# Graph attention, graph convolution and LSTM on one core: the ramp of the attention stage laid out anew, and stores within the last LSTM round

## The chip, the cores and the metric

The kernel runs on one core of a Trainium2 chip. The metric is device time in microseconds (us) of one execution; lower is better.

## What is computed

32 graphs of 256 nodes with 128 features each (fp32, 4.19 MB) share one adjacency matrix. Each of two layers normalises its input and adds its result to it:

```python
h = jnp.maximum(_layernorm(x, axis=-1), 0.0)
x = x + gat(h, adj, W, a)   # e = leaky(s1_i + s2_j), masked by adj, softmax over j, times h W
h = jnp.maximum(_layernorm(x, axis=-1), 0.0)
x = x + gnn(h, adj, Wg0, bg0, Wg1, bg1, Wih, Whh, bih, bhh)
# gnn: two graph convolutions h = relu(adj @ (h Wg + b)); then for p = 1, 2, 3, 4 every run of
# p nodes goes through a p-step LSTM, whose last hidden state replaces the run's last node
```

## The kernel before, in words

All of x stays in SBUF as `xs`, 64 tiles of 128 nodes. The unit of work is a pair of graphs: four tiles, 512 columns; there are 16 pairs (`PAIRS`). PE is the matrix engine, DVE the vector, ACT the scalar engine, POOL is GpSimd, SP issues transfers. Each runs a hand-written program in its own order, and semaphores are all that ties them: a wait holds everything behind it on its engine.

**Attention stage** (`phase_a`). A software pipeline of ticks. In tick t, ACT normalises pair t (L448), PE transposes it (L908), and ACT copies it to `hT` (L474). In the tick behind that, PE makes its products with W (L898) and its scores S (L902, once the scores before are read); DVE masks S by `adj_neg`, takes row maxima (L642) and applies the leaky slope (L674). Two, three and four ticks behind follow the exponentials (ACT L481), the transposes of the probabilities (PE L929), and attention times values (PE L917) with the addition into `xs` (DVE L681, L688). DVE also takes the second layer norm's statistics there (L632).

x comes in by five transfers on SP's queue (`X_GROUPS`, L321), of 8, 8, 16, 16 and 16 tiles. The first layer norm has three steps: statistics on DVE (`first_statistics`, L594, eight tiles at a time: three times ahead of the ticks, once at the end of ticks 0 to 4), `norm_scale` on POOL for a whole group (L357 to L366, ten operations, nine of which POOL waits for itself), and the activation on ACT, which at tick t below 6 waits for `ln_ok` of t+1 pairs and at tick 6 for that of all 16.

At the end of tick 1 DVE splits the transposed adjacency into two parts (`adj_parts`, L610, L611). At the start of tick 3 PE sums its rows into PSUM bank 7 (L885). At the end of tick 2, DVE splits these sums (`row_sum_parts`, L617 to L622), and PE waits for that at tick 4's start. Behind its norms POOL splits the weights of the graph convolution (from L375).

**LSTM rounds.** Graph convolutions and the one-step LSTM (`phase_b`) come next, then ten rounds (`ROUNDS`): four of two steps, four of three, two of four. In a round two chains (`par` 0 and 1) take turns; a step is 12 input products (L937; nine at a round's first step) and, from the second on, 12 recurrent ones (L1036, L1040) behind waits for the two parts of the hidden state. A chain's four gates have a PSUM bank each. ACT applies gates and tanh (L550, L540), DVE does the cell (L812, L814, `cell_sum` L822), the split of the hidden state (L773, L777, L784) and the result's rows (`join` L804, `result_h` L799).

**Output.** Behind the last round PE transposes the results, four tiles a pair, into banks 0 to 3 in turn (L1055), up to three pairs ahead of DVE, which adds a bank to `xs` (`add_pair`, L858). SP (L328) and ACT (L577) store every other pair, 256 KB each.

## Time and profile before

| | us |
|---|---|
| median of three runs (lowest, highest) | 476.65 (476.65, 477.36) |
| the profiled execution | 477.25 |
| its span, first to last instruction | 475.4 |
| busy: PE, DVE, ACT, POOL | 431.2, 382.0, 322.8, 70.7 |

The profiled execution's own time is 1.85 us above its span and 0.60 above the median of the runs. PE is busy for 91% of the span. In the page's forty slices of 11.9 us its lowest tenths are 0, 6 and 5 in the first three, and 7 and 1 in the last two. Times in the trace count from the span's start; the granted clock is a share of PE's full 2.4 GHz.

### The profile page before, as it was taken

What the parts mean: (1) busy time and instruction counts of PE and PEld (TensorE: products, weight loads), DVE (VectorE), ACT (ScalarE), POOL (GpSimd) and SP (SyncE); (2) the same over time, 40 slices, a digit from 0 to 9 for tenths busy, and PEclk for the clock granted to TensorE, in tenths of its full rate; (3) what the DMA queues carried; (4) which work ended last, traced back from release to release, by engine and by line L of the source; (5) the groups of instructions that cost most, each with busy time, mean ns of one, the idle gap of its engine ahead of it and who ended that gap; (6) DMA issues with size and microseconds to landing.
All of it is one profiled execution on the core that took longest, in us unless ns stands there. A gap on an engine that the chain in (4) does not pass through costs nothing.

```text
span 475.4 us, 8063 instructions
## 1 busy us (share of the span) xinstructions
PE 431.2 (91%) x2522; PEld 378.7 (80%) x2522; DVE 382.0 (80%) x985; ACT 322.8 (68%) x630; POOL 70.7 (15%) x163
## 2 busy tenths in 40 slices
PE   0659799997999899999989999999999999999971
PEld 0438688887999798999878888899999988888861
DVE  3599699997868977878777788888788788888883
ACT  0658699987687687887676677767667665585520
POOL 4614853304046500000000000000000000000000
PEclk9998799999999899999999999999999999999986
DMA  8900000000000000000000000000000000000038
GB/s 242 338 18 2 1 1 3 0 0 0 1 2 2 0 0 0 0 0 0 1 0 2 0 1 1 0 1 1 1 1 1 2 0 1 0 0 1 1 106 249
DMA packets 13994, 11.67 MB, mean 25 GB/s; under 512 B 902, under 2 KB 12172, under 8 KB 13708
## 3 DMA queue, kind: packets, MB, share of 16 engines
q1 hardware_dynamic: 8176, 8.39, 5.8%
q10 hardware_dynamic: 5788, 2.91, 2.3%
q8 instruction: 16, 0.26, 0.2%
q14 instruction: 14, 0.11, 0.1%
HBM read 7.10 MB, written 4.19 MB: 24 GB/s over the span
## 4 chain that ended last, share of the span: by engine, by line
PE 72%; DVE 15%; issue 4%; ACT 3%; POOL 2%; DMA 1%; DVEq 1%; ACTq 0%; POOLq 0%
PE ps L937 47%; PE ps L1036 12%; PE ps L1040 6%; DVE score L674 3%; DVE score L642 3%; PE ps L917 3%; DVE xs L688 2%; DVE stats L594 1%; ACT v_norm L448 1%; DVE stats L632 1%; POOL scale L363 1%; ACT work L550 1%; DMA xs<-in_x 1%; PE ps L1055 1%; PE ps L902 1%
## 5 line engine op out<-in xcount | busy, mean ns | idle before, releaser
L550 ACT ACTIVATE work<-ps,bl 128x512 f32<-128x512 f32 (+2 forms) x204 | 111.2, 628 | 26.7 <-PE ps L1040 20.0
L937 PE MATMUL ps<-h_hi,wl_hi 128*128 128x512 f32 (+3 forms) x252 | 94.2, 374 | 3.2 <-DVE h_lo L738 3.2
L937 PE MATMUL ps<-h_lo,wl_hi 128*128 128x512 f32 (+3 forms) x252 | 94.0, 373 | 0.0
L937 PE MATMUL ps<-h_hi,wl_lo 128*128 128x512 f32 (+3 forms) x252 | 93.9, 373 | 0.0
L540 ACT ACTIVATE work<-work 128x512 f32<-128x512 f32 (+2 forms) x56 | 31.5, 570 | 45.4 <-DVE work L822 34.5
L937 PEld LDWEIGHTS ps<-h_hi,wl_hi 128*128 128x128 f32 x252 | 47.5, 189 | 10.5 <-issue 2.0
L448 ACT ACTIVATE v_norm<-xs,shift,scale 128x128 f32 (+1 forms) x128 | 52.8, 492 | 3.9 <-POOL shift L366 3.9
L937 PEld LDWEIGHTS ps<-h_lo,wl_hi 128*128 128x128 f32 x252 | 47.7, 189 | 7.6
L937 PEld LDWEIGHTS ps<-h_hi,wl_lo 128*128 128x128 f32 x252 | 47.7, 189 | 6.8
L1036 PE MATMUL ps<-s_hi,wl_lo 128*128 128x512 f32 (+2 forms) x144 | 51.5, 360 | 0.0
L1036 PE MATMUL ps<-s_hi,wl_hi 128*128 128x512 f32 (+2 forms) x144 | 51.3, 358 | 0.0
L523 ACT ACTIVATE s_hi<-ps 128x512 fp32r<-128x512 f32 x48 | 28.4, 599 | 19.5 <-PE ps L937 16.1
L917 PE MATMUL ps<-wh,pT 128*128 128x130 f32 x256 | 35.6, 296 | 2.7 <-DVE xs L688 2.3
L917 PEld LDWEIGHTS ps<-wh,pT 128*128 128x128 f32 x256 | 32.9, 207 | 5.2 <-issue 2.3
L511 ACT ACTIVATE work<-ps,bl 128x512 f32<-128x512 f32 x48 | 30.9, 682 | 8.9 <-DVE work L712 7.0
L1040 PE MATMUL ps<-s_lo,wl_hi 128*128 128x512 f32 (+2 forms) x144 | 34.0, 358 | 0.3 <-DVE s_lo L784 0.3
L773 DVE TENSOR_TENSOR s_hi<-work 128x512 fp32r<-128x512 f32 (+2 forms) x36 | 22.0, 611 | 12.6 <-ACT work L540 11.8
L481 ACT ACTIVATE prob<-score,ebias 128x256 f32<-128x256 f32 x64 | 27.5, 520 | 5.8 <-DVE ebias L654 5.8
L777 DVE TENSOR_TENSOR work<-work 128x512 f32<-128x512 f32 (+2 forms) x52 | 31.2, 601 | 0.0
L1036 PEld LDWEIGHTS ps<-s_hi,wl_lo 128*128 128x128 f32 x144 | 27.1, 188 | 3.6
L1036 PEld LDWEIGHTS ps<-s_hi,wl_hi 128*128 128x128 f32 x144 | 27.1, 188 | 3.4
L736 DVE TENSOR_TENSOR s_lo<-ps,s_hi 128x512 fp32r<-128x512 f32 x32 | 21.9, 686 | 9.3 <-ACT s_hi L523 9.3
(127 smaller groups left out, 951.3 us busy)
## 6 DMA issues: line engine op xcount, KB each, us to landing
result<-xs SPq DMA_DIRECT2D x8, 256.0 KB, 4.4
result<-xs ACTq DMA_DIRECT2D x8, 256.0 KB, 4.9
xs<-in_x SPq DMA_DIRECT2D x2, 512.0 KB, 5.1
work<-in_w_ih_t SPq DMA_DIRECT2D x1, 1024.0 KB, 11.3
work<-in_w_hh_t SPq DMA_DIRECT2D x1, 1024.0 KB, 9.3
adj_raw<-in_adj ACTq DMA_DIRECT2D x1, 256.0 KB, 8.5
adjT_raw<-in_adj_t ACTq DMA_DIRECT2D x1, 256.0 KB, 10.0
wg_raw<-in_w_gcn ACTq DMA_DIRECT2D x2, 64.0 KB
```

The lines of the kernel that those rows point to most:

```text
L448: ins = nc.scalar.activation(v_norm[:, k, :], xs[:, bass.ds(i, 1), :].rearrange("p o f -> p (o f)"), ACT.Relu, scale=scale[:, which, bass. ...
L481: ins = nc.scalar.activation(prob[:, m, k], score[:, m, k], ACT.Exp, scale=1.0 - SLOPE, bias=ebias[:, m, k:k + 1])
L511: nc.scalar.activation(one_row(g), ps[:, 4 + g, :], ACT.Tanh if g == G else ACT.Sigmoid, bias=bl[:, g:g + 1]).then_inc(one_act, 1)
L523: nc.scalar.activation(dst, ps[:, s - 1, :], ACT.Copy if s in (1, 3) else ACT.Relu).then_inc(b_hi[s], 1)
L540: nc.scalar.activation(lw[:, par, R_TC, 0:cols], lw[:, par, R_C, 0:cols], ACT.Tanh).then_inc(c_act[par], 1)
L550: nc.scalar.activation(lw[:, par, g, 0:cols], ps[:, 4 * par + g, 0:cols], ACT.Tanh if g == G else ACT.Sigmoid, bias=bl[:, (p - 1) * GATES ...
L773: nc.vector.tensor_tensor(hi, shaped(lw[:, par, O, :]), shaped(lw[:, par, R_TC, :]), ALU.mult).then_inc(c_hi[par], 1)
L777: nc.vector.tensor_tensor(row(r, par, R_H), row(r, par, O), row(r, par, R_TC), ALU.mult).then_inc(c_h[par], 1)
L917: ins = nc.tensor.matmul(psA[:, b, ui * (D + 2):(ui + 1) * (D + 2)], pT[:, 2 * b + uj, ui * P:(ui + 1) * P], wh[:, (ph - 4) % 4, 2 * b + u ...
L937: ins = nc.tensor.matmul(dst, a, b, start=start and n_ == 0, stop=stop and n_ == 2)
L1036: nc.tensor.matmul(ps[:, 4 * par + g, 0:cols], part, s_hi[:, par, 0:cols], start=False, stop=False)
L1040: nc.tensor.matmul(ps[:, 4 * par + g, 0:cols], weights(p, 1, g)[0], s_lo[:, par, 0:cols], start=False, stop=True).then_inc(c_gate[par], 1)
```

## The change

- **Loads and norms.** x comes in groups of 4, 4, 8, 16, 16, 16 tiles. `norm_scale` has a fourth scratch array and five of its nine self-waits. POOL makes `ident` first. ACT runs one Relu (`warm`) ahead of everything; its six small bias loads go to SP's queue, behind the LSTM weights.
- **PE** does 12 and 16 transposes of `ident` into bank 7 (`turns`) ahead of its first product and behind it.
- **Statistics.** DVE does the groups up to the first of 16 tiles ahead of the ticks, and the last two within ticks 0 to 3. ACT waits for all norms at tick 7.
- **Adjacency parts** move from DVE to POOL, behind the norm of the first group of 16 tiles. **Row sums:** ACT copies them from PSUM at the end of tick 4 (`rs_read`), POOL splits the copy; PE waits for the copy ahead of the first attention product and for the split only in `phase_b`.
- **Last round** (`END`). Between the input and recurrent products of each of its eight steps, PE transposes one pair of results into a gate bank that is free (`bank_out`); DVE adds it within the round and SP stores it. The last step's recurrent products are split by gates, I and G, then F, then O, each finished with its third product.
- **Behind the round** eight pairs are left, in eight banks. SP stores pairs 0 to 11 whole; of pairs 12 to 15 SP and ACT store a half each. The loops are written out.

```diff
-    X_GROUPS = [(0, 8), (8, 8)] + [(c * QUARTER, QUARTER) for c in range(1, 4)]
+    X_GROUPS = [(0, 4), (4, 4), (8, 8)] + [(c * QUARTER, QUARTER) for c in range(1, 4)]
+    FIRST = 3
...
+WITHIN = PAIRS // 2
+HALVED = 4
+
+def bank_out(q):
+    if q < WITHIN:
+        k, par = divmod(q, 2)
+        return 4 * par + F if k == 0 else 4 * (1 - par) + I
+    return [G, F, O, I][q - WITHIN] if q < WITHIN + 4 else q - WITHIN

...
-    with sp.Fori(0, PAIRS // 2) as q:
-        sp.wait_ge(d_out, q * 2 + 1)
-        sp.dma_start(out_v[:, bass.ds(q * 8, 4), :], xs[:, bass.ds(q * 8, 4), :]).then_inc(stored, 16)
-    sp.wait_ge(stored, 16 * PAIRS)
+    sp.wait_ge(b_zero, 1)
+    for l, b in enumerate((b_gcn0, b_gcn1)):
+        for r in (0, 32, 64):
+            sp.dma_start(b_raw[r:r + 1, l, :], b.rearrange("(o f) -> o f", o=1)).then_inc(gcn_w_in, 16)
+    for q in range(PAIRS - HALVED):
+        sp.wait_ge(d_out, q + 1)
+        sp.dma_start(out_v[:, q * 4:q * 4 + 4, :], xs[:, q * 4:q * 4 + 4, :]).then_inc(stored, 16)
+
+    for q in range(PAIRS - HALVED, PAIRS):
+        sp.wait_ge(d_out, q + 1)
+        sp.dma_start(out_v[:, q * 4:q * 4 + 2, :], xs[:, q * 4:q * 4 + 2, :]).then_inc(stored, 16)
+    sp.wait_ge(stored, 16 * (PAIRS + HALVED))
...
 -    for lo, cnt in X_GROUPS:
+    for c, (lo, cnt) in enumerate(X_GROUPS):
         pool.wait_ge(stats_ok, lo + cnt)
         norm_scale(0, lo, cnt)
+        if c == FIRST:
+            pool.wait_ge(adjT_in, 16)
+            done(nc.gpsimd.tensor_copy(adjT_hi[:, :, :], adjT_raw[:, :, :]))
+            nc.gpsimd.tensor_tensor(adjT_lo[:, :, :], adjT_raw[:, :, :], adjT_hi[:, :, :].bitcast(fp32),
+                                    ALU.subtract).then_inc(adjT_ok, 1)
+
+
+    pool.wait_ge(rs_read, 1)
+    done(nc.gpsimd.tensor_copy(rs_full[:, :].bitcast(fp32r), rs_raw[:, :]))
+    for b in range(2):
+        done(nc.gpsimd.tensor_copy(rs_parts[0:64, b], rs_full[0:64]))
+        done(nc.gpsimd.tensor_copy(rs_parts[96:P, b], rs_full[96:P]))
+        done(nc.gpsimd.tensor_tensor(rs_parts[64:96, b], rs_raw[64:96], rs_full[64:96], ALU.subtract))
+    nc.gpsimd.nop().then_inc(rs_ok, 1)
...
-    act.wait_ge(b_zero, 1)
+    act.wait_ge(ident_ok, 1)
+    nc.scalar.activation(warm[:, :], ident[:, 0:1], ACT.Relu)
...
-                act.wait_ge(ln_ok, t + 1 if t < 6 else PAIRS)
+                act.wait_ge(ln_ok, t + 1 if t < 7 else PAIRS)
...
+        if isinstance(t, int) and t == 4:
+            act.wait_ge(rs_ps, 1)
+            nc.scalar.activation(rs_raw[:, :], ps[:, 7, 0:N], ACT.Copy).then_inc(rs_read, 1)
...
+    for q in range(PAIRS - HALVED, PAIRS):
+        act.wait_ge(d_out, q + 1)
+        act.dma_start(out_v[:, q * 4 + 2:q * 4 + 4, :], xs[:, q * 4 + 2:q * 4 + 4, :]).then_inc(stored, 16)
...
-    first_statistics(0, 0)
-    first_statistics(1, 0)
+    first_statistics(0)
+    first_statistics(1)
...
-    first_statistics(2, 0)
+    first_statistics(2)
     dve.wait_ge(adj_in, 16)
-    done(nc.vector.tensor_scalar(adj_neg[:, :, :], adj_raw[:, :, :], 0.0, MASKED, ALU.is_equal, ALU.mult))
...
+    nc.vector.tensor_scalar(adj_neg[:, :, :], adj_raw[:, :, :], 0.0, MASKED, ALU.is_equal, ALU.mult
+                            ).then_inc(adj_neg_ok, 1)
+    first_statistics(FIRST, 0)
+    first_statistics(FIRST, 1)
...
+        if isinstance(t, int) and t == 1:
+            dve.wait_ge(adj_neg_ok, 1)
...
-        if isinstance(t, int) and t == 1:
-            adj_parts()
-        if isinstance(t, int) and t == 2:
-            row_sum_parts()
-        if isinstance(t, int) and t < 5:
-            first_statistics((t + 5) // 2, (t + 1) % 2)
+        if isinstance(t, int) and t < 4:
+            first_statistics(FIRST + 1 + t // 2, t % 2)
...
-        if (k, par) != (steps_of(r) - 1, 1):
+        if (k, par) != (steps_of(r) - 1, 1) or r == END:
             cell_sum(r, k, par)
...
+
+    def add_pair(q):
+        dve.wait_ge(d_T, q + 1)
+        xq = xs[:, q * 4:q * 4 + 4, :].rearrange("p k f -> p (k f)")
+        nc.vector.tensor_tensor(xq, ps[:, bank_out(q), :], xq, ALU.add).then_inc(d_out, 1)
...
+        if r == END:
+            add_pair(0)
...
                 if p == LAST and k > 0:
                     join(r, k - 1, par)
+                if r == END and (k, par) == (0, 1):
+                    add_pair(1)
+                elif r == END and (k, par) != (LAST - 1, 1):
+                    add_pair(2 * k + par + 1)
                 if (k, par) == (LAST - 1, 0):
                     result_h(r, par)
                 elif (k, par) != (p - 1, 1):
...
+                if r == END and (k, par) == (0, 1):
+                    add_pair(2)
+
+    result_h(END, 1)
+    for q in range(WITHIN, PAIRS):
+        add_pair(q)
...
+    def turns(n_):
+
+        pe.wait_ge(ident_ok, 1)
+        for k in range(n_):
+            nc.tensor.transpose(ps[:, 7, (k % 4) * P:(k % 4 + 1) * P], ident[:, :], ident[:, :])
+
+    turns(12)
     pe.wait_ge(gat_w_in, 32)
     nc.tensor.matmul(ps[:, 0, 0:2], wt[:, :], a12[:, :], start=True, stop=True).then_inc(wa_ps, 1)
-    pe.wait_ge(ident_ok, 1)
+    turns(16)
     pe.wait_ge(wa_ok, 1)
     pe.wait_ge(wext_in, 16)
...
-        if isinstance(t, int) and t == 4:
-            pe.wait_ge(rs_ok, 1)
...
+            if isinstance(t, int) and t == 4:
+                pe.wait_ge(rs_read, 1)
             pe.wait_ge(a_pT, t - 3)
...
+                if isinstance(t, int) and t == 2:
+                    pe.wait_ge(rs_ok, 1)
...
                     if g in seen and (r, k) != (0, 0):
                         pe.wait_ge(c_act[par], a_n - (len(seen) - seen.index(g)) + 1)
+                    if r == END and (k, g) == (1, F):
+                        pe.wait_ge(d_out, par + 1)
+                    if r == END and g == I and 2 * k + par > 2:
+                        pe.wait_ge(d_out, 2 * k + par)
                     ins = product(like_window(ps[:, 4 * par + g, :], r, par), weights(p, 0, g), v, True, k == 0)
                     if k == 0:
                         ins.then_inc(c_gate[par], 1)
+                if r == END:
+
+                    q = 2 * k + par
+                    if q in (0, 4):
+                        pe.wait_ge(c_h[q // 4], h_base[r])
+                    if k > 0:
+                        pe.wait_ge(c_act[1 - par], acts_before(r, k - 1 + par) + 1)
+                    transpose_pair(q)
...
+                    for some in ([[I, G], [F], [O]] if (r, k, par) == (END, LAST - 1, 1) else [gates]):
+                        for g in some:
+                            for part in weights(p, 1, g):
+                                nc.tensor.matmul(ps[:, 4 * par + g, 0:cols], part, s_hi[:, par, 0:cols],
+                                                 start=False, stop=False)
+                        pe.wait_ge(c_lo[par], part_base[r] + k)
+                        for g in some:
+                            nc.tensor.matmul(ps[:, 4 * par + g, 0:cols], weights(p, 1, g)[0],
+                                             s_lo[:, par, 0:cols], start=False, stop=True
+                                             ).then_inc(c_gate[par], 1)
+
+    for q in range(WITHIN, PAIRS):
+        if q == WITHIN:
             pe.wait_ge(c_act[0], a_total - 1)
-        if q == 8:
             pe.wait_ge(c_h[0], h_total)
-        if q == 12:
+        if q == WITHIN + 3:
+            pe.wait_ge(d_out, WITHIN)
+        if q == WITHIN + 4:
             pe.wait_ge(c_h[1], h_total)
-        after(pe, d_out, q - 3, 0)
+        transpose_pair(q)
```

DVE's program ahead of tick 1 and in it, before (the engine's first rows; `x16` is sixteen in a row, L642 and L665 the masked scores):

```order
L594 BN_STATS stats<-xs 128x6 x16
L600 TENSOR_SCALAR wext<-ps 128x1
L601 TENSOR_SCALAR wext<-ps 128x1
L602 COPY wa<-ps 128x128
L594 BN_STATS stats<-xs 128x6 x8
L605 TENSOR_SCALAR adj_neg<-adj_raw 128x512
L594 BN_STATS stats<-xs 128x6 x8
L642 ISA score,m<-ps,adj_neg 128x256
```

and after:

```order
L632 BN_STATS stats<-xs 128x6 x8
L638 TENSOR_SCALAR wext<-ps 128x1
L639 TENSOR_SCALAR wext<-ps 128x1
L640 COPY wa<-ps 128x128
L632 BN_STATS stats<-xs 128x6 x8
L643 TENSOR_SCALAR adj_neg<-adj_raw 128x512
L632 BN_STATS stats<-xs 128x6 x24
L665 ISA score,m<-ps,adj_neg 128x256
```

Ahead of the first scores DVE now has 40 tiles' statistics instead of 32; the last eight are of the group that begins at tile 32, by the fifth transfer of x.

The end of DVE's tick 1 and its start of tick 2, before:

```order
L674 SCALAR_TENSOR_TENSOR score<-ps,wh,score 128x256 x4
L610 CAST adjT_hi<-adjT_raw 128x512
L611 TENSOR_TENSOR adjT_lo<-adjT_raw,adjT_hi 128x512
L594 BN_STATS stats<-xs 128x6 x8
L650 SCALAR_TENSOR_TENSOR low<-m,wh 128x4
```

and after:

```order
L665 ISA m 128x1
L699 SCALAR_TENSOR_TENSOR score<-ps,wh,score 128x256 x4
L632 BN_STATS stats<-xs 128x6 x8
L673 SCALAR_TENSOR_TENSOR low<-m,wh 128x4
L665 ISA score,m<-ps,adj_neg 128x256
```

The two operations on the adjacency are gone from DVE; the seven on the row sums at the end of tick 2 (L617 to L622) are gone in the same way.

PE's last step, from its last input product, before:

```order
L937 MATMUL ps<-h_lo,wl_hi 128x512
L1036 MATMUL ps<-s_hi,wl_hi 128x512
L1036 MATMUL ps<-s_hi,wl_lo 128x512
L1036 MATMUL ps<-s_hi,wl_hi 128x512
L1036 MATMUL ps<-s_hi,wl_lo 128x512
L1036 MATMUL ps<-s_hi,wl_hi 128x512
L1036 MATMUL ps<-s_hi,wl_lo 128x512
L1036 MATMUL ps<-s_hi,wl_hi 128x512
L1036 MATMUL ps<-s_hi,wl_lo 128x512
L1040 MATMUL ps<-s_lo,wl_hi 128x512 x4
L1055 MATMUL ps<-ident,result 128x128 x64
```

and after:

```order
L1037 MATMUL ps<-ident,result 128x128 x4
L1089 MATMUL ps<-s_hi,wl_hi 128x512
L1089 MATMUL ps<-s_hi,wl_lo 128x512
L1089 MATMUL ps<-s_hi,wl_hi 128x512
L1089 MATMUL ps<-s_hi,wl_lo 128x512
L1093 MATMUL ps<-s_lo,wl_hi 128x512 x2
L1089 MATMUL ps<-s_hi,wl_hi 128x512
L1089 MATMUL ps<-s_hi,wl_lo 128x512
L1093 MATMUL ps<-s_lo,wl_hi 128x512
L1089 MATMUL ps<-s_hi,wl_hi 128x512
L1089 MATMUL ps<-s_hi,wl_lo 128x512
L1093 MATMUL ps<-s_lo,wl_hi 128x512
```

Of the 64 transposes behind the last product, 32 are left; four (L1037) now stand in each step of the round.

## Rows read from the trace of the kernel before

**Rows 1.** Stretches: busy us of PE, PEld, DVE, ACT, POOL; clock; DMA share; GB/s

```profile
50.00:60.00 10.00, 7.28 (x38) 6.85 (x39) 4.89 (x22) 7.81 (x17) 8.34 (x26) 0.66 0.00 1
80.00:90.00 10.00, 10.00 (x78) 8.69 (x77) 10.00 (x47) 10.00 (x23) 0.24 (x1) 1.00 0.00 0
440.00:452.00 12.00, 12.00 (x54) 9.74 (x53) 10.56 (x22) 6.55 (x11) 0.00 (x0) 1.00 0.00 1
```

**Rows 2.** Timeline, DVE in the ramp: start, us, line, operation, count, [idle before]

```profile
20.11 0.42 DVE L642 CUSTOM_DVE_ANT_0 score<-ps,adj_neg 128x256 f32<-128x256 f32 x1 [4.29 <-PE ps L902]
...
23.28 0.42 DVE L610 CAST adjT_hi<-adjT_raw 128x512 fp32r<-128x512 f32 x1
...
24.34 1.64 DVE L594 BATCH_NORM_STATS2 stats<-xs 128x6 f32<-128x128 f32 x8
...
29.18 0.41 DVE L617 CAST rs_full<-ps 128x256 fp32r<-128x256 f32 x1
...
31.73 1.65 DVE L594 BATCH_NORM_STATS2 stats<-xs 128x6 f32<-128x128 f32 x8
...
43.14 1.63 DVE L594 BATCH_NORM_STATS2 stats<-xs 128x6 f32<-128x128 f32 x8
...
49.73 0.41 DVE L642 CUSTOM_DVE_ANT_0 score<-ps,adj_neg 128x256 f32<-128x256 f32 x1
...
60.70 0.41 DVE L642 CUSTOM_DVE_ANT_0 score<-ps,adj_neg 128x256 f32<-128x256 f32 x1
```

**Rows 3.** Same timeline, POOL and ACT at the stop at tick 6

```profile
45.26 0.24 POOL L357 TENSOR_TENSOR ln_b<-stats 128x16 f32<-128x16 f32 x1 [6.00 <-DVE stats L594]
...
51.02 1.65 ACT L448 ACTIVATE v_norm<-xs,shift,scale 128x128 f32<-128x128 f32 x4 [3.89 <-POOL shift L366]
51.05 0.40 POOL L375 CAST wg_hi<-wg_raw 128x256 fp32r<-128x256 f32 x1
...
51.53 0.72 POOL L376 TENSOR_TENSOR wg_lo<-wg_raw,wg_hi 128x256 fp32r<-128x256 f32 x1
```

**Rows 4.** Transfer issued at 3.2 to 3.5 us, us to landing

```profile
xs<-in_x SPq DMA_DIRECT2D x1, 0.5 KB, 13.5
```

**Rows 5.** Same timeline, PE's attention products and DVE behind them

```profile
38.61 3.24 PE L917 MATMUL ps<-wh,pT 128*128 128x130 f32 x16
...
41.88 0.18 DVE L681 RECIPROCAL rinv<-ps 128x4 f32<-128x4 f32 x1 [0.26 <-PE ps L917]
...
57.50 0.18 DVE L681 RECIPROCAL rinv<-ps 128x4 f32<-128x4 f32 x1 [1.75 <-PE ps L917]
...
60.84 1.96 PE L917 MATMUL ps<-wh,pT 128*128 128x130 f32 x16
```

**Rows 6.** Same timeline, DVE beside POOL's casts

```profile
54.10 1.66 DVE L674 SCALAR_TENSOR_TENSOR score<-ps,wh,score 128x256 f32<-128x256 f32 x4 [2.45 <-ACT wh L467]
...
150.03 1.11 DVE L748 TENSOR_TENSOR s_lo<-v_norm,s_hi 128x512 fp32r<-128x512 f32 x1
```

**Rows 7.** Timeline of the last LSTM steps and of the output

```profile
448.75 0.69 DVE L812 TENSOR_TENSOR work<-work 128x512 f32<-128x512 f32 x1 [0.50 <-ACT work L550]
...
450.73 0.39 PE L1036 MATMUL ps<-s_hi,wl_hi 128*128 128x512 f32 x1
...
450.76 1.11 DVE L804 TENSOR_TENSOR result<-h_hi,h_lo 128x176 f32<-128x176 f32 x3
...
452.99 2.42 ACT L550 ACTIVATE work<-ps,bl 128x512 f32<-128x512 f32 x4 [1.48 <-PE ps L1040]
...
453.48 1.91 PE L1055 MATMUL ps<-ident,result 128*128 128x128 f32 x16
...
457.00 1.27 DVE L858 TENSOR_TENSOR xs<-ps,xs 128x512 f32<-128x512 f32 x2
...
459.09 8.44 DVE L858 TENSOR_TENSOR xs<-ps,xs 128x512 f32<-128x512 f32 x14
```

**Rows 8.** Busy time by stretch, as rows 1: the stores' last part

```profile
470.00:474.00 4.00, 0.00 (x0) 0.00 (x0) 0.00 (x0) 0.00 (x0) 0.00 (x0) 0.50 0.97 279
```

## What the change does to the time: a prediction

> **What bounds the kernel now.** I read the busy times by stretch first, to find where something is left. In the middle of the attention stage DVE and PE are both busy without a gap, and in the last LSTM steps PE is busy for 12.00 us of 12 at full clock [rows 1]; neither place can give anything. From 50 to 60 us DVE is busy for 4.89 of 10 us at a mean granted clock of 0.66 [rows 1]. So I went on to the timeline of the ramp, to the one of the output, and then to the transfers.
>
> In the ramp DVE hardly stops between its first scores at 20.11 and tick 6 at 49.73; what lies on it there is path. Tick 5 starts when the statistics from 43.14 end, at 44.77, and lasts 4.96 us; tick 6 lasts from 49.73 to 60.70, 10.97 us [rows 2]. ACT's norm of that tick had waited 3.89 us for POOL, which began the last group only at 45.26, when DVE's last first-layer statistics were done [rows 3]. At the other end, the recurrent products of the last step start at 450.73, the first addition of results at 457.00 [rows 7], and the stores then fill the DMA engines (share 0.97, 279 GB/s) until 474 [rows 8]; the span ends at 475.4. The sum is made against the profiled execution, 477.25, which stands 0.60 above the median of 476.65. I call 0.2%, 0.95 us, the least that a measurement of this kernel can tell.
>
> **The ramp, part by part.**
>
> *First scores.* The groups of 4, the five waits fewer in the norm, the early table load and the turns all bring PE's first scores forward. They don't set the new start: ahead of the first scores DVE now has eight statistics of the transfer that lands 13.5 us after an issue at 3.2 to 3.5, at 16.7 to 17.0 [rows 4], and eight take 1.65 [rows 2]. That makes 18.5 where 20.11 stood: **-1.6**. The turns fill bank 7, which nobody reads until the row sums, and end before the first norm; I cost them at nothing. If the transfer came later by one more issue on SP's queue, this term would lose as much.
>
> *Adjacency parts off DVE.* From 23.28 to 24.34: **-1.06** [rows 2]. On POOL the cast and the subtraction of 512 columns cost twice the 256-column rows, 2 x (0.40 + 0.72) = 2.24 [rows 3]. They stand behind the norm of the first 16-tile group. That norm took 5.76 at the stop, from 45.26 to 51.02 [rows 3]; its statistics stand ahead of DVE's wait for the transfer at 16.7 to 17.0, so it ends by 22.8 and the parts by 25. PE wants them at tick 3, which by these terms begins at about 28. Covered.
>
> *Row-sum parts off DVE.* From 29.18 to 31.73: **-2.55** [rows 2]. ACT's copy stands in front of the first attention product; I take **+0.4**, since DVE's cast of the same 256 columns from the same bank took 0.41 [rows 2], with 0 and 0.8 as ends. Behind it on ACT is tick 5's work, on PE the tick's attention, so it is paid once. POOL's split is wanted only some 70 us later.
>
> *One group of statistics fewer behind tick 4.* It moves ahead of tick 1, into the wait for the transfer, already counted above: **-1.63** [rows 2].
>
> *The stop at tick 6.* With the last group counted at the end of tick 3, about 33 by these terms, POOL ends its norm by 39 and ACT wants it at tick 7, at about 48. All of the stop goes: 10.97 - 4.96 = **-6.0**. Sum so far: -1.6 - 1.06 - 2.55 - 1.63 - 6.0 + 0.4 = -12.4.
>
> *What is late next: PE's clock.* PE does its attention products in 3.24 us in the first tick that has them and in 1.96 later [rows 5]. In that first tick DVE waited for them by 0.26, and at the stop, with PE at the lower level again, by 1.75 [rows 5]. After the change PE still has little to do in ticks 1 to 3, so I expect 1.2 GHz when attention starts. For two such ticks the ends are 2 x 0.26 = 0.5 and 2 x 1.75 = 3.5; I take **+1.0**, near the lower end, because 0.26 is the row of the same tick. The ramp: **-11.4**.
>
> *POOL beside DVE.* POOL works for about 4.8 us more beside DVE's ticks (2.24, and the row sums' 2.55 if as fast as on DVE). In the trace, a DVE subtraction of two SBUF tensors took 1.11 beside a cast of POOL [rows 6], and 0.69 for such an operation without POOL [rows 7]; but the ramp's score operation, which reads PSUM, took 1.66 for four beside POOL's casts [rows 6]. I take 0. The Trainium skill (SBUF — State Buffer, Terms) says that the port pair that DVE and GpSimd share is locked for a whole instruction and that the loser stands still; by that alone the moved 4.8 us would come back to DVE. The same skill (GPSIMD Engine Reference, Specifications) restricts it to DVE instructions with two SBUF inputs or in a two-port mode, and the rows 1.11 and 1.66 agree.
>
> **The tail, part by part.** Let S be the start of the last step's recurrent products, 450.73 before; the end was S + 24.67.
>
> *Transposes within the round.* 16 took 1.91 [rows 7], so four take 0.48, and eight steps +3.8 on PE, which has no gap there. DVE waits 0.50 in each step [rows 7], and its addition takes 8.44 / 14 = 0.60 [rows 7]; the step is 0.48 longer, so DVE keeps 0.4 of room. The new wait of PE: an I product waits for the addition two places back. DVE's rows of a step are done at 450.76 + 1.11 = 451.87, the addition then at 452.5, and PE comes to the I product 12 x 0.23 us behind 450.73, at 453.5: 1.0 to spare. Only the first steps, with nine products, can be short; I allow 0.3 (ends 0 and one addition). S moves by +4.1. Behind DVE's wait for the transposes stands the split of the hidden state, which PE wants two steps later.
>
> *The last step.* I and G are finished by the fifth and sixth product instead of the ninth and tenth. ACT's gates start at 452.99, S + 2.26 [rows 7]; four products fewer bring that to S + 1.3. From there two gates take 1.2 (2.42 for four [rows 7]), three operations of the cell about 1.9 (0.69 for one, less when they overlap), `join` 1.1 [rows 7] and `result_h`, of the same three pieces, 1.1. The first of the last eight additions starts at S + 6.6. Before, the first of sixteen started at S + 6.27.
>
> *Stores.* From the first addition to the end it was 475.4 - 457.00 = 18.4. 256 KB at 279 GB/s is 0.94 [rows 8]; eight fewer are 7.5, which leaves 10.9. Additions at 0.60 stay ahead of that. The new end is S + 4.1 + 6.6 + 10.9 = S + 21.6: **-3.1**. The ends are 0 (below) and -4.6, if ACT's and DVE's chain is 1.2 shorter and no step waits. The Trainium skill (DMA: Bandwidth & Descriptors, Anatomy of one DMA) puts a transfer at about 2.0 us plus its bytes at 436 GB/s, an estimate of 0.60 for 256 KB in a full queue. By it the stores would go at the additions' pace and the tail gain 2.7 more. The row, with all engines busy at 279 GB/s, speaks against it.
>
> **Sum.** -11.4 - 3.1 = -14.5; 477.25 - 14.5 = 462.7 for a profiled execution, 0.6 less against the median: **462.1 us**.
>
> **Rivals.**
>
> *PE stays at 1.2 GHz until the pipeline is full*: two ticks at 1.75 instead of 0.5 each, +2.5, 464.6. For: less waiting on DVE leaves PE less time to catch up. Against: 0.26 in the same tick. 14%.
>
> *The tail returns nothing*: PE waits for additions in most steps, or the last chain is no shorter, and what the stores gain the round loses. 465.2, 12%; together with the clock 467.7, 3%.
>
> *More than counted*: no loss by the clock, the tail at its better end, 477.25 - 12.4 - 4.6 - 0.6 = 459.6; were the stores to go at the additions' pace of 0.60, 8 x 0.34 = 2.7 less, 456.9. 14%.
>
> *POOL stops DVE* for the 4.8 us moved there: 466.9. The 1.66 speaks against it. 3%.
>
> *Slower than before.* If DVE's addition comes over 1.0 us later in every step than counted, PE stops in each, and its clock falls inside the round. Its 162 products take 37.4 us at 0.23; at half clock 37 us more, 499 in all. To outweigh 14.5, 40% of the round must run so. No gap in PE's last 12 us and DVE's 0.50 of waiting a step speak against it. 2%.
>
> *The change doesn't do what it says* in one respect already: the early norms shorten nothing, since DVE waits for the transfer at 16.7 to 17.0. That is in the sum.
>
> **How the numbers follow.** The forecast has the remaining 52%, the cases above 48%. All but the last end faster by much over 0.2%: faster 0.97, same 0.01, slower 0.02. The range takes in the better case with its stores and both single losses, and POOL's all but: 457.0 to 466.8. Beyond it lie the two losses together, POOL's case and the slow one, 8%, and what the bounds above miss.
>
> **What would show it.** In the profile after: first scores at about 18.5, behind statistics that wait for a transfer; no adjacency or row-sum work on DVE; ticks of about 5 us up to tick 7 with no stop on POOL, and tick 7 starting at about 49.3, not 60.70; a low clock about tick 4. In the last round, transposes without a gap of PE over 0.3 and one store for each step; behind it, eight additions at 0.6 and stores until 13 us behind the round's last `result_h`. A stop at tick 6 or 7, a PE gap in each step of the last round, or DVE operations stretched beside POOL would show a step of mine wrong, and a time above 467 or below 457 the sum.

## The result, and the profile after

The changed kernel took 464.21 us (median of four runs, 464.01 to 464.43) beside 476.65 before: the ratio is 0.9736, interval 0.9719 to 0.9753, 12.4 us faster. Run again beside the experiments it took 462.47 (462.43 to 463.35) beside 476.75: 0.9701, 0.9687 to 0.9714. Both lie in the range given, the forecast of 462.1 was 2.1 below the first and 0.4 below the second. Where these 1.7 us between two measurements of one kernel come from is part of what follows. The profiled execution after (464.01, span 462.2) is 13.2 us of span shorter than the one before; the forecast for it was 14.5.

The timeline of the changed kernel's ramp, DVE's rows with those of PE and POOL that they hang on (start, duration, engine, line, operation, idle before and what ended it):

```profile
17.50 1.64 DVE L632 BATCH_NORM_STATS2 stats<-xs 128x6 f32<-128x128 f32 x8 [0.71 <-DMA xs<-in_x]
...
19.07 0.41 DVE L665 CUSTOM_DVE_ANT_0 score<-ps,adj_neg 128x256 f32<-128x256 f32 x1
...
22.30 0.61 POOL L401 CAST adjT_hi<-adjT_raw 128x512 fp32r<-128x512 f32 x1
22.35 2.07 PE L930 MATMUL ps<-hT,wa 128*128 128x512 f32 x2 [4.90 <-DVE score L699]
22.99 1.27 POOL L402 TENSOR_TENSOR adjT_lo<-adjT_raw,adjT_hi 128x512 fp32r<-128x512 f32 x1
...
24.46 0.17 DVE L673 SCALAR_TENSOR_TENSOR low<-m,wh 128x4 f32<-128x4 f32 x1 [0.61 <-PE ps L930]
...
29.32 0.15 DVE L673 SCALAR_TENSOR_TENSOR low<-m,wh 128x4 f32<-128x4 f32 x1
...
34.15 0.15 DVE L673 SCALAR_TENSOR_TENSOR low<-m,wh 128x4 f32<-128x4 f32 x1
...
34.39 0.24 POOL L384 TENSOR_TENSOR ln_b<-stats 128x16 f32<-128x16 f32 x1 [4.83 <-DVE stats L632]
...
34.74 2.06 PE L947 MATMUL ps<-wh,pT 128*128 128x130 f32 x16 [0.44 <-ACT rs_raw L543]
...
39.47 0.17 DVE L673 SCALAR_TENSOR_TENSOR low<-m,wh 128x4 f32<-128x4 f32 x1 [0.69 <-PE ps L930]
39.47 0.25 POOL L393 TENSOR_TENSOR shift<-ln_c,scale 128x16 f32<-128x16 f32 x1
...
44.60 0.44 DVE L673 SCALAR_TENSOR_TENSOR low<-m,wh 128x4 f32<-128x4 f32 x1
...
49.86 0.15 DVE L673 SCALAR_TENSOR_TENSOR low<-m,wh 128x4 f32<-128x4 f32 x1
49.93 0.41 DVE L665 CUSTOM_DVE_ANT_0 score<-ps,adj_neg 128x256 f32<-128x256 f32 x1
```

The first scores stand at 19.07 (20.11 before [rows 2]), tick 7 at 49.93 (60.70 [rows 2]): 10.8 us won in the ramp, where the forecast had 11.4. POOL's last norm ends at 39.7 and no longer stops anyone ([rows 3] show the stop). The L673 rows at the start of ticks 2 to 7 give the lengths of ticks 2 to 6: 4.9 from 24.46, then 4.8, 5.3, 5.1 and 5.3.

Between tick 7 and the last step's recurrent products lay 390.0 us before (60.70 [rows 2] to 450.73 [rows 7]) and 395.8 after (49.93 to 445.75 below): 5.8 longer, where the round alone was to be 4.1 longer. From there to the end it was 24.7 and is 462.2 - 445.75 = 16.4. So 10.8 - 5.8 + 8.2 = 13.2.

From the same timeline, further places: DVE's 13th, 14th and 16th reciprocal of the attention stage (L706, one for each pair; they serve as landmarks below) with PE's products between them, PE's rows at the first LSTM steps and in the last round, and the gates and additions behind it:

```profile
98.41 0.17 DVE L706 RECIPROCAL rinv<-ps 128x4 f32<-128x4 f32 x1
...
100.12 3.31 PE L947 MATMUL ps<-wh,pT 128*128 128x130 f32 x16 [2.11 <-DVE xs L713]
...
103.47 0.18 DVE L706 RECIPROCAL rinv<-ps 128x4 f32<-128x4 f32 x1 [1.02 <-PE ps L947]
...
114.93 0.17 DVE L706 RECIPROCAL rinv<-ps 128x4 f32<-128x4 f32 x1
...
147.01 0.49 PE L967 MATMUL ps<-h_hi,wl_hi 128*128 x1 [1.81 <-DVE h_lo L759]
...
232.14 0.50 PE L967 MATMUL ps<-h_hi,wl_hi 128*128 128x512 f32 x1 [1.41 <-DVE h_lo L759]
...
418.53 0.48 PE L967 MATMUL ps<-h_hi,wl_hi 128*128 128x512 f32 x1 [0.75 <-DVE xs L848]
...
421.40 0.60 PE L1037 MATMUL ps<-ident,result 128*128 128x128 f32 x4
...
445.75 0.47 PE L1089 MATMUL ps<-s_hi,wl_hi 128*128 128x512 f32 x1
...
447.19 2.43 ACT L596 ACTIVATE work<-ps,bl 128x512 f32<-128x512 f32 x4 [1.01 <-PE ps L1093]
...
452.32 4.85 DVE L848 TENSOR_TENSOR xs<-ps,xs 128x512 f32<-128x512 f32 x8
```

And its busy time by stretch (columns as [rows 1], the first number behind the stretch its length):

```profile
100.00:102.00 2.00, 1.88 (x11) 1.91 (x12) 1.29 (x5) 0.60 (x2) 1.77 (x6) 0.66 0.00 0
102.00:104.00 2.00, 2.00 (x11) 2.00 (x11) 0.98 (x7) 1.71 (x4) 2.00 (x1) 0.50 0.00 0
...
148.00:150.00 2.00, 2.00 (x7) 1.53 (x7) 1.97 (x3) 1.39 (x3) 1.85 (x4) 0.61 0.00 0
456.00:458.00 2.00, 0.00 (x0) 0.00 (x0) 1.16 (x2) 0.00 (x0) 0.00 (x0) 1.00 1.04 287
460.00:462.20 2.20, 0.00 (x0) 0.00 (x0) 0.00 (x0) 0.00 (x0) 0.00 (x0) 0.50 0.59 171
```

Behind a pause of 2.11 us the clock falls to 1.2 GHz (0.50) and the attention products take 3.31 us. Before, the same products behind a pause of the same length took 2.03, at full clock:

```profile
110.83 2.03 PE L917 MATMUL ps<-wh,pT 128*128 128x130 f32 x16 [2.11 <-DVE xs L688]
```

From the 13th to the 16th reciprocal it is 16.52 us after and was 15.37 before. These 1.15 and the 4.6 by which the round is longer (34.70 before, 39.31 after, from the round's first input product to the last step's recurrent ones) make the 5.8 between tick 7 and the last step.

### The profile page after: what moved, and what is told of

It is laid out like the page before. It is cut to its first block, busy times and chain, and to the rows that moved or that the text cites. A ratio compares the mean times of both kernels' runs of the same rounds, so it can differ in the third digit from the quotient of the medians.

```text
span 462.2 us, 8017 instructions
## 1 busy us (share of the span) xinstructions
PE 433.5 (94%) x2550; PEld 380.9 (82%) x2550; DVE 379.4 (82%) x976; ACT 322.9 (70%) x632; POOL 77.6 (17%) x182
## 3 DMA queue, kind: packets, MB, share of 16 engines
HBM read 7.10 MB, written 4.19 MB: 24 GB/s over the span
## 4 chain that ended last, share of the span: by engine, by line
PE 69%; DVE 18%; ACT 4%; issue 3%; DMA 3%; DVEq 1%; SPq 1%; ACTq 0%
PE ps L967 47%; PE ps L1089 11%; PE ps L1093 6%; DVE score L699 4%; DVE score L665 3%; DMA xs<-in_x 3%; DVE xs L713 3%; DVE stats L655 2%; PE ps L947 2%; ACT v_norm L491 1%; ACT work L596 1%; DVE xs L848 1%; PE ps L1011 1%; ACT prob L524 1%; PE ps L1007 1%
## 5 line engine op out<-in xcount | busy, mean ns | idle before, releaser
L586 ACT ACTIVATE work<-work 128x512 f32<-128x512 f32 (+2 forms) x56 | 31.5, 570 | 44.3 <-DVE work L843 33.6
L947 PE MATMUL ps<-wh,pT 128*128 128x130 f32 x256 | 33.9, 287 | 3.0 <-DVE xs L713 2.5
L947 PEld LDWEIGHTS ps<-wh,pT 128*128 128x128 f32 x256 | 31.1, 196 | 5.7 <-issue 2.9
```

Source lines behind the costliest of these rows:

```text
L586: nc.scalar.activation(lw[:, par, R_TC, 0:cols], lw[:, par, R_C, 0:cols], ACT.Tanh).then_inc(c_act[par], 1)
L947: ins = nc.tensor.matmul(psA[:, b, ui * (D + 2):(ui + 1) * (D + 2)], pT[:, 2 * b + uj, ui * P:(ui + 1) * P], wh[:, (ph - 4) % 4, 2 * b + u ...
```

## The experiments

Each was run five or six times beside the kernel before. The first four rows come from one chip, the next four from a second, the last four from a third; medians compare within four rows. The ratio is of runs taken side by side and can differ from that of the medians by some tenths of a per cent.

| kernel | us, median (lowest, highest) | ratio to before (interval) |
|---|---|---|
| ramp alone | 465.91 (464.54, 466.94) | 0.9763 (0.9743, 0.9782) |
| output alone | 473.83 (473.15, 475.22) | 0.9941 (0.9923, 0.9959) |
| before, wait one tick later | 472.32 (470.16, 472.60) | 0.9887 (0.9866, 0.9908) |
| changed, first pause filled | 462.56 (462.01, 463.33) | 0.9701 (0.9684, 0.9719) |
| filled, no turns | 461.62 (461.27, 463.14) | 0.9677 (0.9654, 0.9701) |
| filled, start as before | 463.37 (462.37, 463.66) | 0.9703 (0.9682, 0.9724) |
| filled, adjacency parts on DVE | 461.50 (461.26, 461.63) | 0.9668 (0.9649, 0.9688) |
| filled, row sums copied in tick 3 | 461.57 (460.88, 462.84) | 0.9670 (0.9647, 0.9694) |
| changed, again | 462.47 (462.43, 463.35) | 0.9701 (0.9687, 0.9714) |
| both pauses filled | 463.58 (462.88, 464.51) | 0.9726 (0.9713, 0.9740) |
| both, copy in tick 3, warm scores | 462.60 (461.40, 463.31) | 0.9701 (0.9687, 0.9715) |
| both, whole stores | 462.96 (461.61, 464.40) | 0.9712 (0.9691, 0.9732) |

**The two halves apart.** The first kernel has the changed ramp and the output as before, the second the reverse.

> The change without its output part: loads, norms, statistics, adjacency parts and turns as changed, the last round and the stores as before. Theory (the two halves don't meet, and the change lost about 1.1 us at the end of the attention stage to a lower clock that the new ramp brings with it): tick 7 of the attention stage starts 10.8 us earlier than before, the last round 9.6 earlier, 476.65 - 9.6 = 467.0, with the first attention product behind PE's 2.11 us pause at 100 us again at about 3.3 us instead of 2.0. Rival (the output part brings the loss in the middle with it): 465.9 and 2.0.

> The output part of the change alone on the kernel before. Theory: the round 4.7 us longer, the time from the last step's recurrent products to the end 8.2 shorter, 476.65 - 3.5 = 473.1, one pause of PE of about 0.75 us in the round's fourth step. Rival (the tail's gain needs the ramp's new order, or is only 3.1 or less): 473.6 or more.

10.8 us and 2.9 us by medians, 13.6 together; the whole change won 12.4 in the first measurement and 14.3 in the second. The output alone shows the same one pause of 0.75 in the round; in its trace the round is 4.6 longer and the end 7.9 shorter. Its median of 473.83 lies on the rival's side (473.6 or more) and its lowest run, 473.15, at the theory's 473.1: the time doesn't part the two. By the trace it is 3.3, between the theory's 3.5 and the rival's 3.1; that the tail's gain needs the new ramp is ruled out, since the ramp here is as before. The ramp alone agrees with the rival by its time, but not for the rival's reason. Its timeline has the same pause of PE:

```profile
101.17 2.03 PE L928 MATMUL ps<-wh,pT 128*128 128x130 f32 x16 [2.11 <-DVE xs L696]
```

and its busy time by stretch full clock behind it:

```profile
102.00:104.00 2.00, 2.00 (x20) 2.00 (x19) 1.93 (x10) 0.85 (x3) 1.91 (x3) 1.00 0.00 0
```

The output part does nothing at that place, and the ramp alone brought no fall there in this execution. Nor does the whole change always bring one. Its second profile has the same pause, and full clock behind it; the rows are the 13th reciprocal, the products and the 16th reciprocal:

```profile
98.51 0.17 DVE L706 RECIPROCAL rinv<-ps 128x4 f32<-128x4 f32 x1
...
100.23 2.03 PE L947 MATMUL ps<-wh,pT 128*128 128x130 f32 x16 [2.11 <-DVE xs L713]
...
113.83 0.17 DVE L706 RECIPROCAL rinv<-ps 128x4 f32<-128x4 f32 x1
```

That is 15.32 us instead of 16.52. So the fall belongs to an execution, not to a part of the change, and the two halves add up as far as the spread lets one see.

**One number.** The kernel before, with ACT's wait for all norms a tick later and nothing else:

```diff
-                        act.wait_ge(ln_ok, t + 1 if t < 6 else PAIRS)
+                        act.wait_ge(ln_ok, t + 1 if t < 7 else PAIRS)
```

> The kernel before with one number changed: ACT waits for all norms at tick 7 instead of tick 6. Theory (the stop at tick 6 is this wait alone: POOL ends at 50.99 and ACT would ask a tick later, at about 52): the stop of 6.0 us goes whole, 476.65 - 6.0 = 470.7, though the statistics stand where they stood. Rival (the stop only moves: POOL is late at tick 7 too, so the earlier statistics are needed): 475 to 476.

Its timeline, POOL's last norm and DVE's first operation of ticks 6 and 7:

```profile
46.22 0.24 POOL L357 TENSOR_TENSOR ln_b<-stats 128x16 f32<-128x16 f32 x1 [6.99 <-DVE stats L594]
...
50.61 0.15 DVE L650 SCALAR_TENSOR_TENSOR low<-m,wh 128x4 f32<-128x4 f32 x1
...
55.57 0.15 DVE L650 SCALAR_TENSOR_TENSOR low<-m,wh 128x4 f32<-128x4 f32 x1
```

Tick 6 takes 4.96 us instead of 10.97, though POOL starts the last norm about as late as before (46.22, 45.26 [rows 3]). The stop goes whole. By medians the time gains 4.4: in the profiled execution ticks 3 and 4 lost 1.0 of the 6.0 to a PE at the lower level, with DVE waiting 0.61 and 0.51 for it. So about a third of the whole change's gain hangs on one number. The earlier statistics, which the forecast gave the 6.0 to together with the wait, look like a second cure for the same stop: in the profile after, POOL's last norm ends at 39.72, and ACT's norm of tick 6 starts only at 42.15. The changed kernel with the wait back at tick 6 was not run.

**The pause filled.** Twelve transposes of the identity on PE at the start of tick 17:

```diff
+                if isinstance(t, int) and t == 17:
+                    for k in range(12):
+                        nc.tensor.transpose(psT[:, (k % 4) * P:(k % 4 + 1) * P], ident[:, :], ident[:, :])
                 if live(4):
```

> The changed kernel with 12 transposes of the identity on PE at tick 17's start, inside its 2.11 us pause at 98 to 100 us, into a bank nobody reads. Theory (the granted clock fell to 0.50 behind that pause, as it did not before the change, and this costs 1.1 us): the attention products there take 2.0 instead of 3.3 us and the time is 464.2 - 1.1 = 463.1. Rival (the loss there is not the clock's, or the clock falls for the ramp's sake): 464.2. If the transposes are themselves in the way: above 464.5.

The same place in its timeline, first the fill and then the attention products:

```profile
97.19 1.47 PE L940 MATMUL ps<-ident 128*128 128x128 f32 x12
99.47 2.03 PE L950 MATMUL ps<-wh,pT 128*128 128x130 f32 x16 [0.80 <-DVE xs L713]
```

Full clock behind it, 2.03 instead of 3.31. The time from the 13th to the 16th reciprocal is 16.52 in the two profiles with a fall there, the first one after and the one-number kernel's. In the four other profiles with the pause open it is 15.32 to 15.37, and in all eight with the pause filled 15.31 to 15.48. So a fall costs 1.1 to 1.2. The 14th reciprocal alone would mislead: up to it the one-number kernel has lost only 0.45 and the profile after 1.05. No fall was seen behind the fill, but two falls in six profiles without it and none in eight with it could be chance: that the fill prevents a fall is not shown. By its time alone the kernel can't be told from the changed one on the third chip (0.9701 both), where the profiled execution had no fall to lose at that place.

**Landmarks in the ramp.** The next four kernels differ by little more than their times spread, so they are compared from the first scores to the fourth and to the fifth reciprocal. From the fifth to the twelfth all profiles of the changed ramp take the same, 34.8 to 34.9. The first row has the six profiles of kernels with one and the same ramp; what lies within it can't be told from chance.

| kernel | first scores at | to the fourth | to the fifth |
|---|---|---|---|
| same ramp, six profiles | 18.16 to 19.48 | 34.26 to 34.57 | 39.52 to 40.18 |
| of these, first pause filled | 18.43 | 34.26 | 39.52 |
| filled, no turns | 18.35 | 34.25 | 39.84 |
| filled, start as before | 20.56 | 33.47 | 38.52 |
| filled, adjacency parts on DVE | 18.46 | 34.86 | 39.90 |
| filled, row sums copied in tick 3 | 18.77 | 33.84 | 39.88 |

**The parts of the start.** These four start from the kernel with the first pause filled. Without the 28 transposes of the start:

> The kernel of the filled pause, without the 28 transposes of the identity at the start. Theory (the first scores wait for DVE's statistics of the fifth transfer, not for PE): PE's first scores end up to 1 us later, about 16, still ahead of 19; the time stays within 0.5 of 462.6. Rival (the turns keep PE at full clock where it counts): slower by 1 or more, and a lower clock in ticks 1 and 2 than with them.

PE's first scores end at 15.65, about where the theory had them, and DVE's first scores stand where they stood. Up to the fourth reciprocal it is 34.25 us, with the turns 34.26: no worth of the turns shows. The time, 461.62, is lower than the theory's 462.6, which came from another chip. Then the whole start as before the change:

```diff
-    X_GROUPS = [(0, 4), (4, 4), (8, 8)] + ...
-    FIRST = 3
+    X_GROUPS = [(0, 8), (8, 8)] + ...
+    FIRST = 2
...
-            nc.scalar.activation(warm[:, :], ident[:, 0:1], ACT.Relu)
...
-            turns(12)
...
```

> The kernel of the filled pause with the whole start as before: groups of 8 and 8, nine waits in the norm, no early table load, no turns; DVE's statistics, the adjacency, the row sums and ACT's wait as changed. Theory: the first scores then wait for PE again, at about 20.1 as before instead of 19, and the time is 462.6 + 1.0 = 463.6. Rival (they are worth nothing, the transfer hides all of it): 462.6. Rival (they are worth all of the first term and more): 464.2 or above.

DVE's timeline, the statistics behind the transfer and the first scores:

```profile
16.99 1.64 DVE L629 BATCH_NORM_STATS2 stats<-xs 128x6 f32<-128x128 f32 x8 [0.83 <-DMA xs<-in_x]
20.56 0.42 DVE L661 CUSTOM_DVE_ANT_0 score<-ps,adj_neg 128x256 f32<-128x256 f32 x1 [1.92 <-PE ps L925]
```

DVE waits 1.92 for PE again. From the start of the statistics behind the transfer to the fourth reciprocal it is 37.0 us here, and 35.8 to 36.1 in the same-ramp profiles and without turns: the groups of 4, the shorter norm and the early table load (ACT's load of 1.28 us starts at 5.88 in the profile after, at 11.40 before) are worth about 1 together. Up to the fifth reciprocal 0.4 to 1.0 of it is left. The time, 463.37, is near the theory's 463.6. The forecast's first term stands on both legs: PE's early scores and the transfer.

**Adjacency parts back on DVE**, the same two operations at the end of tick 1:

> The kernel of the filled pause with the adjacency's two operations back on DVE at the end of tick 1. Theory of the sum (what leaves DVE's path is won): slower by 1.06. Rival (in tick 2 DVE waits for PE's cold scores by 0.6 anyway, and the work fills part of that): slower by 0.4 to 0.6.

DVE's timeline at the end of tick 1 and the start of tick 2:

```profile
21.61 0.41 DVE L717 CAST adjT_hi<-adjT_raw 128x512 fp32r<-128x512 f32 x1
22.06 0.69 DVE L719 TENSOR_TENSOR adjT_lo<-adjT_raw,adjT_hi 128x512 fp32r<-128x512 f32 x1
...
24.22 0.14 DVE L669 SCALAR_TENSOR_TENSOR low<-m,wh 128x4 f32<-128x4 f32 x1
```

DVE now has no wait in front of the L669 row: the work fills the 0.61 that it otherwise waits for scores that PE makes at the lower clock. Up to the fourth reciprocal it is 34.86, 0.6 more than 34.26 and 0.3 more than the longest of the same-ramp profiles; up to the fifth, 39.90 lies within them. So it costs 0.3 to 0.6 where it stands, near the rival's 0.4 to 0.6, and no loss is shown further on. The whole time, 461.50, shows none either; more on that at the end of this section.

**Row sums copied a tick earlier** (`t == 4` becomes `t == 3` at ACT's copy):

> The kernel of the filled pause with ACT's copy of the row sums at the end of tick 3 instead of tick 4. Theory (in tick 4 PE waited 0.44 us for the copy and DVE had the wait an operation later): faster by 0.4, PE's first attention product waits for no copy. Rival (the copy only delays ACT's work one tick earlier): the same.

33.84 up to the fourth reciprocal, 0.4 less, as expected; L673 in tick 5 waits 0.45 instead of 0.69. But up to the fifth it is 39.88, and nothing is left of the gain. Between the two, L673 took 1.22 us beside POOL's casts of the adjacency; the kernel with the first pause filled alone has the same row at 54.18 with 0.32:

```profile
52.61 0.17 DVE L706 RECIPROCAL rinv<-ps 128x4 f32<-128x4 f32 x1
...
54.09 1.22 DVE L673 SCALAR_TENSOR_TENSOR low<-m,wh 128x4 f32<-128x4 f32 x1
...
58.65 0.16 DVE L706 RECIPROCAL rinv<-ps 128x4 f32<-128x4 f32 x1
```

The time, 460.88 to 462.84, is too wide for 0.4.

**The changed kernel again, and three more.** The second fill puts 12 transposes at tick 5 of `phase_b`, ahead of the one-step LSTM's first products; the third kernel also puts 32 into tick 2 in front of the scores; the fourth stores the last four pairs whole.

```diff
                         pe.wait_ge(wl_ok, 1)
+                        for k in range(12):
+                            nc.tensor.transpose(ps[:, 5, (k % 4) * P:(k % 4 + 1) * P], ident[:, :], ident[:, :])
```

> The changed kernel as it is, beside the next three on the same chip. Theory (the granted clock falls at PE's pauses of 2.11 and 1.81 us near 100 and 147 us in some executions and not in others, each fall worth about 1.05 us, and the landing of x moves the start by some tenths): the executions lie between 462 and 465, in steps of about 1. Rival (both falls belong to this kernel): all within 0.3 of 464.2.

> The changed kernel with 12 transposes of the identity in each of PE's two pauses, the one ahead of tick 17's attention products and the one ahead of the first products of the one-step LSTM. Theory: full clock behind both in every execution, 2 x 1.05 less than an execution with both falls: 462.1, and what is left of the spread is the landing of x. Rival (the second fall costs nothing, since ACT and DVE are behind there too): as with the first pause filled alone, 462.6.

> Both pauses filled; the row sums copied at the end of tick 3; and 32 transposes of the identity on PE in tick 2 ahead of its scores, where PE waits 4.9 us for DVE. Theory: 0.4 less by the copy and 0.6 less by scores at full clock, 1.0 less than with both pauses filled alone, about 461.1; the scores of tick 2 take 1.0 to 1.2 instead of 2.07 and DVE doesn't wait for them. Rival (the filling itself holds the scores up): the same as with both pauses filled, or slower.

> Both pauses filled, and the last four pairs stored whole, two by SP and two by ACT in turn. Theory (the tail is bound by bytes, 2.1 MB at 285 to 295 GB/s, and the halves only let both queues share the last pair): slower by 0 to 0.4 than with both pauses filled. Rival (the halves are what brought the tail below the forecast by 1.0): slower by 0.8 to 1.0.

The second fill was put in the wrong place. Its 12 transposes ran at 121 us, where PE has no gap, and the pause of 1.80 stood untouched behind them. The timeline of the kernel with both fills:

```profile
121.25 1.47 PE L985 MATMUL ps<-ident 128*128 128x128 f32 x12
...
146.92 0.49 PE L970 MATMUL ps<-h_hi,wl_hi 128*128 x1 [1.80 <-DVE h_lo L759]
```

They cost 1.3 us (33.4 from the 16th reciprocal to that pause's end, 32.1 without), so the kernel is slower than the changed one, and these three times say nothing on the second pause. Compared with each other the three kernels still tell something. With 32 transposes in tick 2 and the copy a tick earlier, the time is 1.0 less by medians than with both fills alone (463.58 to 462.60), as the theory had it. Tick 2 started without a wait; the fourth reciprocal came 33.6 behind the first scores instead of 34.5 and the fifth 38.7 instead of 39.8, below all same-ramp profiles. With the copy alone the fourth was at 33.8, so up to there warm scores add only 0.2; what is won between the fourth and the fifth hangs on L673 and L677 beside POOL again. And with whole stores the end lies 9.7 behind the start of PE's last transposes of pairs 12 to 15 (451.44 to 461.1), with halves 9.7 (451.41 to 461.1): the halves are worth nothing. By medians whole stores are 0.6 faster, within the spread.

**The second pause, from the traces.** From the start of PE's products behind the pause of 1.8 (147.01 after) to the start behind the next one (232.14) it is 85.13 to 85.20 in eight of the fourteen profiles and 84.08 to 84.19 in six. The changed kernel has 85.13 with a clock of 0.61 in the stretch from 148 (in the busy times after, above); adjacency on DVE has 84.10 and full clock:

```profile
145.53 0.49 PE L972 MATMUL ps<-h_hi,wl_hi 128*128 x1 [1.80 <-DVE h_lo L761]
...
229.63 0.50 PE L972 MATMUL ps<-h_hi,wl_hi 128*128 128x512 f32 x1 [1.41 <-DVE h_lo L761]
```

So this is such a fall, about 1.05, at a second place. Before had it here and not at the first pause, the first profile after at both, the changed kernel's second one here only. The three kernels with the misplaced second fill are among the six without; what these 12 transposes, 24 us ahead of the pause, have to do with it is open. The changed kernel's second profile in the same stretch:

```profile
148.00:150.00 2.00, 2.00 (x8) 1.71 (x8) 1.97 (x3) 0.63 (x1) 1.85 (x3) 0.50 0.00 0
```

This is also why the whole time can't show half a microsecond: on the second chip the profiles of no turns (84.08) and of adjacency parts on DVE (84.10) had no fall here, those of the other two kernels (85.13 and 85.15) had one. Of the 1.7 us between the two measurements of the changed kernel the profiles explain the 1.1 by which their spans differ: the second one has the first scores 0.5 earlier and 1.2 less at the first pause, against 0.6 more between the first scores and the fifth reciprocal. The mean granted clock fits, 0.978 in all four runs of the first measurement and 0.980 to 0.985 in the second; where the clock fell is known only of the profiled ones. What decides whether it falls, the runs don't settle. The pauses have the same length to 0.03 in all; the start of everything moves with the landing of x's fifth transfer, behind which DVE's statistics started between 16.5 and 17.9 in the eleven profiles that have them there.

## Why the prediction was right, and where it missed

The forecast beside the profiled execution, in us:

| stretch | forecast | measured |
|---|---|---|
| first scores | -1.6 | -1.0 |
| tick 1 (adjacency parts) | -1.1 | -0.4 |
| tick 2 (row sums) | -2.5 | -2.5 |
| ticks 3 to 5 (statistics, copy, PE's clock) | -0.2 | -1.1 |
| tick 6 (the stop) | -6.0 | -5.7 |
| first pause of PE | none | +1.15 |
| last round | +4.1 | +4.6 |
| from the last step's recurrent products to the end | -7.2 | -8.2 |
| all | -14.5 | -13.2 |

Ticks 2 to 6 took 7.4, 5.0, 6.4, 5.0 and 11.0 us before, from one first operation of a tick (L650) to the next. Most of the mechanisms held. That the sum came as near as it did is in part luck: the 1.0 allowed for PE's clock did not come where it was put, and nearly pays for the fall that was not foreseen. The same goes for the forecast's 0.4 beside the second measurement.

*First scores.* Right in kind: they follow the statistics that wait for the transfer. Forecast 18.5, measured 19.07, since the statistics started at 17.50 and not at 16.85. The landing varies by more than that between executions. Wrong is the sentence that the early norms shorten nothing: with the start as before, DVE waits 1.92 for PE, the first scores stand at 20.56, and about 1 us is lost.

*Adjacency parts.* The step said 1.06. Tick 1 got 0.4 shorter, and with the parts back on DVE 0.3 to 0.6 is lost up to the fourth reciprocal. What failed is the point that only DVE's queue counts there: in tick 2 DVE waits for PE's scores, 2.07 us behind 4.90 of idle, and 0.61 of the term went into that wait. On POOL they took 1.88 instead of 2.24, and ended at 24.3 against 25.

*Row sums.* Right: 2.55 forecast, tick 2 is 2.5 shorter (7.4 to 4.9). The copy's +0.4 is the 0.44 that PE waits at 34.74. The kernel with the copy a tick earlier won it back up to the fourth reciprocal, and lost it again to L673 beside POOL.

*Statistics and stop.* Right in size: the statistics of tick 4 and the stop are gone, and tick 6 takes 5.26 instead of 4.96 since L673 takes 0.44 in it. The step let the last group be counted earlier and ACT want it later, and needed only the second: ACT's wait alone removes the stop.

*PE's clock.* The size was near, the place was wrong. I put +1.0 on the first attention products; they ran at 2.06, full clock. The lower level came at tick 2's scores instead (0.61), and at the end of the attention stage (1.15), of which the prediction had nothing: its first sentences took the stage from tick 7 on as fixed. This is the term that failed. The pause of 2.11 stands in the trace before, at full clock; I did not read it, and that trace alone could not have told that the clock sometimes falls there.

*POOL beside DVE.* Taken as nothing; it is 0.7 in the profile after, and 0.7 to 1.4 in the eleven profiles with a changed ramp, while the profile before has none. L673 and L677, small operations with two SBUF inputs, stretch from 0.15 to 0.44 beside POOL here, and once to 1.22; the operations that read PSUM keep their 1.66. The Trainium skill (GPSIMD Engine Reference, Specifications) names contention of the two engines for DVE instructions with two SBUF inputs, and the rows agree. It is not the 4.8 us of the rival. But which of these operations meet POOL shifts from execution to execution, and that is much of the spread in the ramp.

*The round.* 8 x 0.48 and 0.3 were forecast; measured are 0.75 in the one pause and 4.6 in all. The prediction allowed a wait only in the first steps, the two with nine products; the pause stands ahead of the fourth step. There PE waits for the addition of pair 2, 417.70 to 418.4, which stands on DVE behind the second chain's first cell and the split of its hidden state.

*The last step and the stores.* First addition at 452.32, 6.6 behind 445.75, as forecast. From there to the end 9.9 instead of 10.9. The 2.1 MB take 7.3 at the 287 GB/s of the stretch from 456, which leaves 2.6 around them; before, 4.19 MB took 15.0 at 279 [rows 8], with 3.4 of the 18.4 around them. Why 0.8 less stands around them was not tested, except that the halves have no part in it. The Trainium skill's 436 GB/s (DMA: Bandwidth & Descriptors, Anatomy of one DMA; fitted there to transfers that GpSimd issues, while SP and ACT issue these) is not seen: the DMA share is 1.04 at 287.

## What to carry to other kernels

Undo a stop at both its ends before you credit one: a single number in a wait was worth 4.4 of 12.4 us here. Work that leaves a busy engine is worth only what that engine does not then wait, so look one operation further, at whoever feeds it. Read pauses of PE of about two microseconds as a risk of their own. And measure in stages, from one landmark of the trace to the next, because total times of single microseconds hide which part won; choose landmarks behind which all runs go alike, and profile one kernel several times to see what a difference must exceed. Here a gain of 0.4 at the fourth reciprocal was gone at the fifth.

## What the runs showed that I had not expected

PE's pauses of 2.11 and 1.8 us, equal to 0.03 us in all profiles and at the same place of the program, let the granted clock fall to 0.50 in some executions and not in others, for 1.05 to 1.2 us each: two of six at the first pause where it was open, eight of fourteen at the second. With 12 transposes in the first one none of eight had a fall, too few to show that they prevent it. The landing of x, which moves by up to 1.4 us between executions, and DVE's small operations beside POOL, up to 0.7, are other parts of the spread. What decides a fall stays open, and so does a fill in the right place of the second pause, which was not tried.
